# Sixteen attention heads a batch: the second attention's contexts summed already turned, its row sums from ScalarE, the first attention's heads two to a slot, in new instruction sequences

## What is computed

```python
    x = x + _L0_xattn_ref(_layernorm(x, axis=-1), ctx_1024, ctx_1024, mask_BxS2_if1, L0_xattn_Wq, L0_xattn_bq, L0_xattn_Wk, L0_xattn_bk, L0_xattn_Wv, L0_xattn_bv, L0_xattn_Wo, L0_xattn_bo)
    x = x + _L0_ffn_ref(_layernorm(x, axis=-1), L0_ffn_Ws1, L0_ffn_Ws2, L0_ffn_W1, L0_ffn_W2, L0_ffn_Wr)
    x = x + _L1_xattn_ref(_layernorm(x, axis=-1), ctx_1024, mask_Bx1xSxS2_ff0, L1_xattn_wq, L1_xattn_wk, L1_xattn_wv, L1_xattn_wo)
    x = x + _L1_ffn_ref(_layernorm(x, axis=-1), L1_ffn_q_w, L1_ffn_k_w, L1_ffn_v_w, L1_ffn_o_w, L1_ffn_sel_v_w, L1_ffn_sel_o_w, L1_ffn_route_scale)
```

```python
        logits = jnp.einsum('btnh,bfnh->bnft', k, q)
        logits = logits + bias
        weights = jax.nn.softmax(logits, axis=-1)
        attn = jnp.einsum('bnft,btnh->bfnh', weights, v)
        return jnp.einsum('bfnh,nhd->bfd', attn, wo)
```

## Time and profile before

| | us |
|---|---|
| median of three runs | 1483.8 |
| the profiled execution | 1481.03 |
| its span, first to last instruction | 1479.2 |
| TensorE busy in the span | 1404.5 (95%) |
| VectorE | 1283.9 (87%) |
| ScalarE | 1275.8 (86%) |
| GpSimd | 859.0 (58%) |

### The profile page before, as it was taken

How to read it: one execution, slowest core, us unless ns; L and a number is a source line. 1 busy time by engine, 2 the same in 40 slices (tenths; PEclk the granted TensorE clock), 3 DMA queues, 4 the chain that set the end, 5 groups by cost and what they waited for, 6 DMA issues and landing times.

```text
span 1479.2 us, 34876 instructions
## 1 busy us (share of the span) xinstructions
PE 1404.5 (95%) x9748; PEld 963.9 (65%) x9905; DVE 1283.9 (87%) x5266; ACT 1275.8 (86%) x4428; POOL 859.0 (58%) x1345
## 2 busy tenths in 40 slices
PE   4678999999999999999999999999999999999998
PEld 2455666666676666667666666766666676666654
DVE  3677988998998999899899999989999998998886
ACT  3657888899988889998888999888899988889886
POOL 3113656556565656656565565656556565655567
PEclk8689999999999999999999999999999999999999
DMA  4410000000000000000000000000000000000000
GB/s 136 139 56 16 10 14 16 15 15 12 15 11 14 16 15 15 12 15 11 14 16 15 15 13 15 11 14 16 15 15 13 15 11 14 14 15 7 8 3 4
DMA packets 68960, 30.18 MB, mean 20 GB/s; under 512 B 19168, under 2 KB 68768, under 8 KB 68768
## 3 DMA queue, kind: packets, MB, share of 16 engines
q1 hardware_dynamic: 51552, 19.31, 4.9%
q10 hardware_dynamic: 17216, 8.65, 2.1%
HBM read 17.31 MB, written 2.10 MB: 13 GB/s over the span
## 4 chain that ended last, share of the span: by engine, by line
PE 62%; ACT 13%; DVE 11%; POOL 7%; issue 4%; SPq 2%; DMA 1%; POOLq 0%; ACTq 0%; another core or an unknown queue 0%; DVEq 0%
PE psC L309 43%; PE psA L309 7%; PE psB L309 6%; DVE nmA L2240 5%; ACT PTA L1344 3%; ACT PS L1344 3%; POOL accO L3405 3%; DVE PTB L2365 3%; ACT TE L1344 3%; DVE TE L2497 2%; ACT PTB L1344 2%; SPq L3776 2%; PE psA L421 1%; POOL accO L3413 1%; PE psB L553 1%
## 5 line engine op out<-in xcount | busy, mean ns | idle before, releaser
L3405 POOL TENSOR_TENSOR accO<-accO,TE 128x512 f32<-128x512 f32 x192 | 246.3, 1283 | 143.9 <-DVE TE L2497 137.7
L1344 ACT ACTIVATE TE<-psC,gate 128x128 f32<-128x128 f32 x1024 | 300.1, 406 | 17.7 <-PE psC L309 10.4
L1344 ACT ACTIVATE TE<-psC,gateO 128x128 f32<-128x128 f32 x1024 | 292.5, 375 | 24.8 <-PE psC L309 16.2
L2497 DVE SCALAR_TENSOR_TENSOR TE<-psC,gate,TE 128x128 f32<-128x128 f32 x1024 | 284.5, 339 | 29.5 <-PE psC L309 18.4
L2497 DVE SCALAR_TENSOR_TENSOR TE<-psC,gateO,TE 128x128 f32<-128x128 f32 x1024 | 287.1, 341 | 13.2 <-PE psC L309 8.2
L3393 POOL TENSOR_TENSOR TE<-TE 128x256 f32<-128x256 f32 x256 | 192.4, 752 | 164.5 <-DVE TE L2497 160.4
L309 PE MATMUL psC<-Vh,xTh 128*128 128x512 f32 x512 | 263.3, 514 | 2.3 <-ACT PS L1344 1.2
L309 PE MATMUL psC<-Oh,ch 128*128 128x512 f32 x512 | 262.9, 513 | 0.2
L309 PE MATMUL psC<-Oh,cl 128*128 128x512 f32 x512 | 203.0, 396 | 0.0
L309 PE MATMUL psC<-Vh,xTl 128*128 128x512 f32 x512 | 202.5, 396 | 0.0
L309 PE MATMUL psC<-Ol,cb 128*128 128x512 bf16 x452 | 176.2, 390 | 0.0
(11 more groups left out here) (228 smaller groups left out, 3426.7 us busy)
## 6 DMA issues: line engine op xcount, KB each, us to landing
bdB<-Kc SPq DMA_DIRECT2D x384, 16.0 KB
raw<-in_L_ffn_v_w ACTq DMA_DIRECT2D x8, 512.0 KB, 4.5
raw<-in_L_ffn_o_w ACTq DMA_DIRECT2D x8, 512.0 KB, 4.2
x_sb<-in_x SPq DMA_DIRECT2D x32, 64.0 KB, 2.1
ctx_sb<-in_ctx SPq DMA_DIRECT2D x32, 64.0 KB, 2.0
bdA<-Kc SPq DMA_DIRECT2D x128, 8.0 KB
Qb<-Qc SPq DMA_DIRECT2D x128, 8.0 KB
bias_sb<-in_mask_Bx1xSxS_ff SPq DMA_DIRECT2D x32, 64.0 KB, 1.9
```

The source lines that it names most:

```text
L1344: return A.activation(o, i, func, **kw)
L2497: m = V.scalar_tensor_tensor(TE[:, i, e], psC[:, p, e * P:(e + 1) * P], gates[:, e:e + 1], TE[:, i, e], ALU.mult, ALU.add)
L3405: G.tensor_tensor(accO[:], TE[:, slot(b, H1)] if h == 1 else accO[:], TE[:, slot(b, H1 + h)], ALU.add).then_inc(o_fe, 1)
```

## The change

- Second attention, row sums: b_exp's four exps now have accum_out, into denB. VectorE's b_attend(0) takes the reciprocals of denB. GpSimd's new b_spread writes each of them 8 times side by side (rdB8), TensorE's b_spread transposes that, and ScalarE's b_spread copies it to SBUF (rdTB).
- Second attention, contexts: the values of a head stand in V1 in 32 columns, of which 8 are the head's and 24 are zero, at a different place for each t. b_pvs sums over t into one 128x128 block of psB, which so comes out with the hidden dimension on the partitions. VectorE's b_attend(1) multiplies it with rdTB into atTB. b_unnorm, b_ut and b_att are gone.
- First attention: two heads share a slot. The stationary operand V0 has 18 columns for a head: its own 8 and the ones, and 9 zero columns in the place of its partner; a_pvs sums two groups into one block. UA has 256 columns instead of 512, and a_ut makes 2 transpositions instead of 4. The weights are permuted once, at the start, to fit.
- a_stats2 and a_norm2 have statistics of their own (stA2, mvA2, rsA2).
- The sequences of all five engines are new, in start(), period(i) and end().

The diff of the steps, cut to its core; of the sequences TensorE's loop alone, around the new step:

```diff
...
-        UA = sb("UA", [P, NT * P])
+        UA = sb("UA", [P, 2 * P])
...
-        Vaug = sb("Vaug", [P, NH, HD + 1])
+        V0 = sb("V0", [P, 2 * (NH + 1) * (HD + 1)])
+        V0_heads = V0[:].rearrange("p (k x) -> p k x", k=2)[:, :, 0:NH * (HD + 1)].rearrange(
+            "p k (g s) -> p k g s", g=NH // 2)
...
-        Vaug1 = sb("Vaug1", [P, NH, HD + 1])
+        V1 = sb("V1", [P, NT * (NJ * SLOT + HD)])
+        V1_heads = V1[:].rearrange("p (t x) -> p t x", t=NT)[:, :, 0:NJ * SLOT].rearrange(
+            "p t (j s) -> p t j s", j=NJ)[:, :, :, 0:HD]
         nmB = sb("nmB", [P, NT, NJ])
         PTB = sb("PTB", [P, NT, NJ, P])
-        rdB = sb("rdB", [P, NH])
-        atB = sb("atB", [P, NH, HD])
+        denB = sb("denB", [P, NJ, NT])
+        rdB = sb("rdB", [P, NJ * NT])
+        rdB8 = sb("rdB8", [P, NJ * NT, HD])
+        rdTB = sb("rdTB", [P, P])
         atTB = sb("atTB", [P, P])
...
-                        m = mm(psA[SLOT * j:SLOT * j + HD + 1, 0, t * P:(t + 1) * P], Vaug[:, NJ * t + j, :],
-                               PTA[:, t, j, :])
+                        r, k = t // 2, t % 2
+                        n = (k * NH // 2 + r * NJ + j) * 2 * (HD + 1)
+                        m = mm(psA[SLOT * j:SLOT * j + 2 * (HD + 1), 0, r * P:(r + 1) * P], V0[:, n:n + 2 * (HD + 1)],
+                               PTA[:, t, j, :], k == 0, k == 1)
                 m.then_inc(a_pv, 1)
...
-                for t in range(NT):
-                    m = T.transpose(psA[:, 1, t * P:(t + 1) * P], UA[:, t * P:(t + 1) * P], ident)
+                for r in range(2):
+                    m = T.transpose(psA[:, 1, r * P:(r + 1) * P], UA[:, r * P:(r + 1) * P], ident)
                 m.then_inc(a_utr, 1)
...
+            def b_spread(b):
+                if b not in BATCHES:
+                    return
+                pe.wait_ge(b_rd, b + 1)
+                pe.wait_ge(b_c, 4 * b + 4)
+                T.transpose(psB[:, 1, 0:P], rdB8[:].rearrange("p n d -> p (n d)"), ident).then_inc(b_rt, 1)
...
                     for j in range(NJ):
-                        m = mm(psB[SLOT * j:SLOT * j + HD + 1, 0, t * P:(t + 1) * P], Vaug1[:, NJ * t + j, :],
-                               PTB[:, t, j, :])
+                        n = (NJ * t + j) * SLOT
+                        m = mm(psB[SLOT * j:SLOT * (j + 1), 0, 0:P], V1[:, n:n + SLOT], PTB[:, t, j, :], t == 0, t == NT - 1)
...
-
-            def b_ut(b):
-                if b not in BATCHES:
-                    return
-                pe.wait_ge(b_u, b + 1)
-                pe.wait_ge(b_c, 4 * b + 4)
-                for t in range(NT):
-                    m = T.transpose(psB[:, 1, t * P:(t + 1) * P], Qh1f[:, t * P:(t + 1) * P], ident)
-                m.then_inc(b_utr, 1)
-
-            def b_att(b):
-                if b not in BATCHES:
-                    return
-                pe.wait_ge(b_at, 2 * b + 2)
-                T.transpose(psB[:, 1, 0:P], atB[:].rearrange("p n d -> p (n d)"), ident).then_inc(b_attr, 1)
...
             def b_exp(b, t):
                 if b not in BATCHES:
                     return
                 act.wait_ge(b_nm, 4 * b + t + 1)
+                act.wait_ge(b_at, b)
                 for j in range(NJ):
-                    m = copy(PTB[:, t, j], PTB[:, t, j], ACT.Exp, bias=nmB[:, t, j:j + 1], scale=-1.0)
+                    m = copy(PTB[:, t, j], PTB[:, t, j], ACT.Exp, bias=nmB[:, t, j:j + 1], scale=-1.0,
+                             accum_out=denB[:, j, t:t + 1])
                 m.then_inc(b_e, 1)
...
-                copy(UA[:], psA[:, 0, :]).then_inc(a_u, 1)
+                copy(UA[:], psA[:, 0, 0:2 * P]).then_inc(a_u, 1)
...
-            def b_unnorm(b):
-                if b not in BATCHES:
-                    return
-                act.wait_ge(b_pv, b + 1)
-                act.wait_ge(b_qs, b + 1)
-                copy(Qh1f, psB[:, 0, :]).then_inc(b_u, 1)
-
-            def b_att(b):
-                if b not in BATCHES:
-                    return
-                act.wait_ge(b_attr, b + 1)
-                copy(atTB[:], psB[:, 1, 0:P]).then_inc(b_atT, 1)
+            def b_spread(b):
+                if b not in BATCHES:
+                    return
+                act.wait_ge(b_rt, b + 1)
+                act.wait_ge(b_atT, b)
+                copy(rdTB[:], psB[:, 1, 0:P]).then_inc(b_rs8, 1)
...
             def b_attend(b, n):
                 if b not in BATCHES:
                     return
-                o = psB[:, 1, :].rearrange("p (n w) -> p n w", n=NH)
-                dve.wait_ge(b_utr, b + 1)
                 if n == 0:
-                    V.reciprocal(rdB[:], o[:, :, HD]).then_inc(b_at, 1)
-                    return
-                dve.wait_ge(b_at, 2 * b + 1)
-                dve.wait_ge(b_attr, b)
-                V.tensor_tensor(atB[:], o[:, :, 0:HD], along(rdB[:], HD), ALU.mult).then_inc(b_at, 1)
+                    dve.wait_ge(b_e, 4 * b + 4)
+                    dve.wait_ge(b_rd, b)
+                    V.reciprocal(rdB[:], denB[:].rearrange("p j t -> p (j t)")).then_inc(b_at, 1)
+                    return
+                dve.wait_ge(b_pv, b + 1)
+                dve.wait_ge(b_rs8, b + 1)
+                dve.wait_ge(b_o, b)
+                V.tensor_tensor(atTB[:], psB[:, 0, 0:P], rdTB[:], ALU.mult).then_inc(b_atT, 1)
...
+            def b_spread(b):
+                if b not in BATCHES:
+                    return
+                pool.wait_ge(b_at, b + 1)
+                pool.wait_ge(b_rt, b)
+                G.tensor_copy(rdB8[:], along(rdB[:], HD)).then_inc(b_rd, 1)
...
                 values(i - 4, 1, 0)
+                a_scores2(i - 1, 3)
+                b_spread(i - 2)
+                b_pvs(i - 2)
                 c_scores(i - 3, 1)
-                a_scores2(i - 1, 3)
-                b_pvs(i - 2)
                 a_pvs(i - 1)
                 values(i - 4, 2, 1)
                 a_ut(i - 1)
-                b_ut(i - 2)
                 values(i - 4, 2, 0)
                 a_att(i - 1)
                 values(i - 4, 3, 1)
...
```

1279 lines of the change are left out of this document (643 added, 636 removed).

## The result

The changed kernel takes 1517.1 us (median of 4 runs, 1515.9 to 1518.9), the kernel before 1483.2 us, run beside it: ratio 1.0231, 95% interval 1.0213 to 1.0249. It is slower, as forecast, but by 34 us and not by 11; the time lies above the range of 1463 to 1512. The profiled execution spans 1515.2 us against 1479.2.

The account below looks back on a forecast made before the run. The prediction took ScalarE's gap-free run plus TensorE's return path to bound each period. +0.72 - 0.19 = +0.53 us, times 27 = +14.3, with the start +11.3, gave 1495 us as median; range 1463 to 1512.

Parts of the forecast that it names:

- the comparison within the PSUM kind: On ScalarE, c_exp with reads every 0.34 us against PSUM copies without at 0.2525: a read costs 0.0875.
- Rival A: On ScalarE, the read hides in an SBUF exp's longer start: period changes by -0.11, 1478 us; chance 0.20.
- the credit: Savings on ScalarE and TensorE set against the reads: 0.48 and 0.20 of copies, 0.19 behind the run.
- 1.40 - 0.48 - 0.20: ScalarE's gap-free run: reads added, copy into Qh gone, copy into UA halved; +0.72 us a period.
- the return path: TensorE behind ScalarE's run: b_att gone, 0.13, and fewer changes between matmul kinds, 0.06; -0.19 us a period.
- b_spread adds a transposition (0.13) inside the run, covered by ScalarE: On TensorE, the new 0.13 us transposition lies under ScalarE's work and adds nothing to the period.
- no step crosses its two ends: ScalarE's work is reordered only within its gap-free run, so the run changes by just +0.72 us.
- The run's own length: ScalarE's gap-free stretch from outputs(6) to c_exp(1), 18.64 us a period, grows by 0.72.
- Start and end: Before and behind the repeated periods, b's unhidden chain gets shorter: -3 us, between 0 and -6.
- Rival B: ScalarE's run stops ending last and TensorE bounds: 0.71 us a period saved, 1462 us; chance 0.16.
- Rival C: First attention's keys and queries arrive late, a_scores(0) waits 0.8 us a period: 1517 us; chance 0.10.
- Contexts: On TensorE, larger weight loads of b_pvs and a_pvs: 0.2 us inside ScalarE's run, at most 0.9, outside the sum.

Follow-up runs that it names:

- before_reads: The kernel before with only the 16 accumulator reads a batch added to the second attention's exponentials: 1529.2 us, ratio 1.0315.
- old_spread_later: The changed kernel's instructions in the old sequences, with b_spread behind b_pvs on TensorE: 1510.1 us, ratio 1.0191.
- old_order2: The changed kernel's instructions in the sequences of the kernel before, with b_spread put in ahead of b_pvs: 1523.2 us, ratio 1.0280.
- spread_later: The changed kernel, new sequences, with b_spread moved behind b_pvs on TensorE: 1515.7 us, ratio 1.0237.
- first_only: The kernel before with the first attention's part of the change alone, old sequences: 1474.4 us, ratio 0.9955.
- queue_start: The changed kernel with the start of SyncE's queue in the order of the kernel before: 1511.9 us, ratio 1.0208.
- first_values_up: The kernel before with the first attention's part alone, and values(0, 1) moved ahead of b_trans(0) on TensorE: 1506.8 us, ratio 1.0175.
- first_bias_up: The kernel before with the first attention's part alone, and b_bias(2) moved ahead of a_max(0) on VectorE: 1474.2 us, ratio 0.9948.

## Why the prediction was right and wrong, step by step

**The sign and the size of the read were right.** The prediction took 0.0875 us for a read, 1.40 a period, by the comparison within the PSUM kind. The rows show 0.09 within b_exp, and adding the reads alone to the kernel before costs 1.53 us a period. Rival A (0.0475) is out: nothing of the read hides in the longer start of an SBUF exp.

**The step that failed is the credit, "1.40 - 0.48 - 0.20" and the "-0.19" of the return path.** Forecast was +1.40 for the reads and -0.87 for all else; measured are +1.53 for the reads, put alone into the kernel before, and 1.10 - 1.53 = -0.43 for all else. The sum needs all of ScalarE's run and what follows it to be one path, before and after. One way through the runs sizes the terms one by one, each as a difference of two periods: reads +1.53 (before_reads less before), the saved copies and transpositions -0.67 (old_spread_later less before_reads), b_spread's place +0.46 (old_order2 less old_spread_later), the new sequences -0.22 (changed less old_order2). Together +1.10, the measured change. Forecast were +1.40, -0.87, 0 and 0. The terms don't add freely. By way of spread_later the last two come out otherwise, +0.16 for the new sequences and nothing that can be told for b_spread's place; with the reads taken out of the changed kernel, the reads are 0.88 and all else +0.22. In none of these does the credit of 0.87 come out. So:

- The credit was 0.20 too large even with b_spread out of the way, and its working was wrong as well. The prediction put the copy into Qh on the path and called the 0.65 us of turnings hidden under c_exp(1), because TensorE waits 0.3 us for PS. The chain has it the other way round: UA, the turning of UA, the turning of Qh. That wait was real but didn't set the period: first_only has it too (2.8 us in 9 waits) while its chain has nothing of ScalarE. And another path was level, TensorE's own loop, at which first_only stops with 0.19 of 0.42. In the changed kernel the chain passes neither UA nor the end of the run at all.
- The prediction's question for b_spread went to GpSimd's copy (0.46 if its cover is gone, and costed at nothing). In the old order the cost came on TensorE: b_spread ahead of b_pvs adds the wait for the last turned row block ahead of 24 matmuls that don't need it. "b_spread adds a transposition (0.13) inside the run, covered by ScalarE" is the sentence that fails. That its price is 0.46 as well is chance. In the new order the same wait costs nothing that can be told, since ScalarE's run is level with it.
- The new order was taken as neutral inside the run ("no step crosses its two ends"). It is not: with it the reads cost 0.57 us less than the 1.45 of the old order (0.88), and without reads it costs 0.35. The net of these is the -0.22. Which part of the new order does either stays open.

**The run's own length was right**, +0.78 against +0.72. The sign of being wrong that the prediction named, gaps in the run or no growth, did not come either. A forecast of a window can hold while the forecast of the period falls: the crossing from ScalarE to TensorE had moved from the end of the run to b_exp(1).

**Start and end**: forecast -3, measured +6.0 ahead of batch 5 and +1.3 behind the last UA. The saved work of b was counted, SyncE's new start sequence was named and not costed. It holds the first scores back by 4.5 us, of which 2.6 are left at batch 5 (queue_start). The reads are another 1.6: without them batch 5's UA comes at 232.35 instead of 233.95. If the two add, 1.8 of the 6.0 stay open. The two ends are 10.3 of the 24.7 us by which the difference of the spans was missed (36.0 against 11.3); the repeated part is the other 14.3 (28.6 against 14.3).

**Rival B** (TensorE bounds, 1462) needed the chain on TensorE all round and 42.4 us. In the changed kernel the chain leaves it for 5.8 us of exps in most periods. Without the reads it is on TensorE for 560 of the 600 us between 500 and 1100, on VectorE for 24, and the period is still 43.35. So B's 42.4 isn't reached there either; the wait of a_scores(0) for Qb is part of that, the rest stays open.

**Rival C** gave 1517 and 44.4 us, and 1517.1 and 44.23 came. That is luck. Its wait is there, but it is 0.2 us in most periods of the changed kernel and at most 0.6 (the start of a_scores(0) behind the matmul ahead of it, less 0.23), not 0.8. With the reads out, moving the call back costs 0.9 us a period.

**Contexts.** The loads grew to 109 ns at 32 columns and 97 at 18 (groups by form, 600 to 1000 us; count, busy us, mean ns), which is 0.83 and 0.78 ns a column from the 90 ns at 9, where 0.86 was the estimate. The Trainium skill ("TensorE: Matmul & The Clock Gate", Part 2, step 1) states that a load's timing scales with its column count; the trace agrees for the growth, but the loads aren't in proportion to their columns, as 90 ns stand at 9 of them already.

```profile
...
L327 PEld LDWEIGHTS psB<-PTB,V 128*32 128x32 f32 x288 | 7.3, 109 | 1.1
...
L327 PEld LDWEIGHTS psA<-PTA,V 128*18 128x18 f32 x288 | 7.1, 97 | 3.3 <-issue 3.3
```

The 32 matmuls of b_pvs take 806.24 - 805.23 = 1.01 us instead of 0.90, so 0.11 of the 32 x 0.019 = 0.6 us by which the loads grew comes out, and the rest overlaps. The 0.2 taken was near.

## What to carry to other kernels

A saving is worth its size only until the next path, and in this kernel that path was level: of 0.42 us saved by first_only, 0.19 came out. So before subtracting savings from a cost, ask of each which path it lies on, and read the chain of waits beside the list of waits: the chain named b_ut, the list a wait that set nothing. The chain itself names one of several level paths. And when an instruction is put into an order, ask what its own wait holds back on its engine, not only how long it takes: b_spread's 0.1 us of transposition cost 0.46 by its place in the old order. Moving a call because of a visible wait gave nothing or lost 23 to 32 us in five of six trials here. In the worst of them, first_values_up, the moved call had no buffer yet, so look at what the moved call itself waits for, and not only at the hole that it fills.

## What the runs showed of the hardware

An accumulator read behind an exp on ScalarE costs the same 0.09 us with an SBUF source as with a PSUM one, and 0.096 in the period when the run is the path. A weight load of TensorE took 90, 97, 109 and 192 ns at 9, 18, 32 and 128 columns of f32.

The kernel's best time found is 1474 us, with the first attention's part of the change alone (first_only and first_bias_up); with the second attention's part and its 16 reads, no order tried was faster than 1510 us.
